# A residual plus bias, made by VectorE in attention and read back in feed-forward

## Chip, cores, metric

The program runs on one core of one Trainium2 chip. Its time is the device time of one execution in microseconds (us), lower is better. The engines are named as in the profile: PE is TensorE (PEld its weight loads), DVE is VectorE, ACT is ScalarE, POOL is GpSimd, SP is SyncE, which only issues DMAs; "SPq" rows are those issues.

## What is computed

A chain of four graph layers over 50000 nodes and 25000 edges, each followed by a residual and a normalization. The change touches the first layer alone, a graph transformer, and of it the end of the feed-forward part:

```python
scores = jnp.sum(q[src] * k[dst], axis=-1) / math.sqrt(D) + edge_bias
# softmax over the edges of each dst, weighted sum of v, out @ oW + ob
x = layer_norm(x + out, ln1_g, ln1_b)
h = x @ f1W + f1b
h = jax.nn.gelu(layer_norm(h, lnf_g, lnf_b), approximate=False)
h = h @ f2W + f2b
x = layer_norm(x + h, ln2_g, ln2_b)      # layer_norm(x, g, b) = (x - mu) * rsqrt(var + EPS) * g + b
...
x = _layernorm(x + _L0_gnn_ref(x, ...), axis=-1)
```

The last line adds the chain's input x to the layer's result. Since ln2_b is added last in that result, the kernel adds x + ln2_b (called xb) in one step: z = u * inverse + xb, where u is the centred row times ln2_g.

## The kernel before

Rows have 128 features. A tile is 512 rows, held as 128 partitions x 4 x 128 floats (256 KB). There are NT = 98 tiles of nodes and ET = 50 tiles of edges. The passes run one after the other: prepare (lists by counting), attention (attention_pass, about 110 to 768 us), feed-forward (ffn_pass, to about 1768 us), then back1, mean1, three gated layers and mean3, which the change leaves alone.

Every pass has one hand-written program for each engine. Within a pass, `over_tiles(engine, tiles, lag, step)` calls `step` once for each number `now`, and `tile_at(k)` in it is tile `now - k`; each engine carries out its step in the order in which it is written, and semaphore counts tie the engines together. `t.slot4` is the buffer n % 4, and a wait for a count of `t.n - 3` says that tile n - 4 has freed this buffer. `wait_alone` is the same wait ahead of a DMA issue, and everything that stands behind it on SyncE's queue stands still with it.

**Attention.** In step `now`, SyncE loads the list of edge ends of tile now (`idx`, L1261), edge features of tile now - 1 and cut of now - 2; the waits ahead of these concern buffers used some four tiles earlier. GpSimd issues eight gathers for tile now (L1282: four times 128 rows for the source, four for the destination), once idx has landed and the rows of tile now - 2 have been transposed by TensorE. TensorE transposes the rows, and in the next step makes q, k and v; VectorE in step `now` handles five stages of five tiles: the maxima of tile now - 3 (L1366 to L1379), the product q * k of tile now - 1 (L1385), att of now - 5 (L1392), sums of now - 3 (L1397 to L1409) and the output addition of now - 6 (L1416). Ahead of the loop SyncE loads eleven small weights of attention and then, by `up.load`, eleven for feed-forward, among them `up_idx`, the list of 98 x 4 pointers a partition, which is stored in HBM in runs of four integers.

**Feed-forward.** In step `now`, GpSimd issues four gathers (L1561), adds x and ln2_b for tile now - 10 (L1572), and raises the variances of four norms to the power -1/2 in one instruction (L1584), for which it waits for VectorE's L1717; VectorE's step has thirteen kinds of instructions, of them z (L1690), the only reader of xb. SyncE loads x of tile now and, a second time, x of tile now - 8 (`xr`, L1546), the latter once xb of tile now - 10 is made.

## Time and profile before

| | us |
|---|---|
| median of three timed runs | 5799.37 (5794.79 to 5803.73) |
| profiled execution | 5761.92 |
| its span | 5760.1 |
| attention, first gather to the start of feed-forward | 130.0 to 768.7 |
| feed-forward, its start to the next pass | 768.7 to about 1769.8 |
| busy over the span | PE 4126.6, DVE 3940.5, POOL 3502.3, ACT 2805.2 |

The profiled execution is 37 us shorter than the median. Shares over the whole span say little here, since the passes have different limits; each stage has to be read by itself, from windows and from the timeline. Where a timeline row carries "[4.25 <-POOL ...]", its engine had stood idle that long, and what is named came last; "issue" names nothing, and "remote" is a releaser that the records don't identify.

### The profile page before, as it was taken

To read this page: it belongs to the slowest core of one execution; us is meant where nothing else is said; L and a number is where in the kernel's file an instruction comes from. 1 tells how busy PE (TensorE), PEld (TensorE's weight loads), DVE (VectorE), ACT (ScalarE), POOL (GpSimd) and SP (SyncE) were. 2 spreads that over 40 slices of the span, in tenths; PEclk is the share of its full clock that TensorE was granted. 3 is DMA by queue.
4 is the path that set the end of the run, shared out by engine and by line. 5 is a ranking of instruction groups with operands and counts; after the bars stand their busy time and mean duration, and the time that the engine had idled before them with its cause. 6 is when DMAs were issued, how large, how long until landed. Compare 5 with 4: busy or idle time off the path is not lost. (4 is left out here: it accounts for less than half of the span.)

```text
span 5760.1 us, 75385 instructions
## 1 busy us (share of the span) xinstructions
PE 4126.6 (72%) x16190; PEld 2465.0 (43%) x16190; DVE 3940.5 (68%) x13570; ACT 2805.2 (49%) x6338; POOL 3502.3 (61%) x3137
## 2 busy tenths in 40 slices
PE   5666659999995555466564779967997669846644
PEld 3233335555552333355443445534443334346643
DVE  6567669999996444377774785557665888846643
ACT  0344437887782100076664445534444555536644
POOL 4677658888876888645556660056104757865456
PEclk8788879999997777777887999989998999978876
DMA  6233323333323444556664775457545666657621
GB/s 224 69 85 86 80 70 111 111 111 111 114 94 76 62 62 62 73 184 192 200 195 145 199 212 139 128 179 218 162 141 155 187 170 209 206 175 231 201 81 60
DMA packets 785242, 802.39 MB, mean 139 GB/s; under 512 B 138080, under 2 KB 551848, under 8 KB 784666
## 3 DMA queue, kind: packets, MB, share of 16 engines
q1 hardware_dynamic: 428922, 393.84, 23.9%
q0 software_dynamic: 117504, 209.42, 14.9%
q10 hardware_dynamic: 238368, 194.32, 10.0%
q8 instruction: 140, 2.29, 0.2%
q14 instruction: 308, 2.52, 0.1%
HBM read 445.32 MB, written 351.92 MB: 138 GB/s over the span
## 5 line engine op out<-in xcount | busy, mean ns | idle before, releaser
L476 PE MATMUL gate_bank<-gate_ht,gate_whh 128*128 128x512 f32 x1764 | 887.0, 618 | 61.2 <-DVE gate_n L546 36.1
L953 POOL DMA_INDIRECT xh<-mean_xh,node_pos x392 | 378.0, 964 | 323.2 <-DVE mean_xh L1009 173.0
L476 PEld LDWEIGHTS gate_bank<-gate_ht,gate_whh 128*128 128x128 f32 x1764 | 329.4, 198 | 465.8 <-issue 375.3
L2147 PE MATMUL back_ps_sums<-back_same,back_rows 128*128 128x512 f32 x400 | 287.2, 884 | 288.6 <-DMA back_rows<-x_a,back_idx 288.5
L1561 POOL DMA_INDIRECT ffn_rows<-att_sums,up_idx x392 | 395.0, 1008 | 109.0 <-issue 108.2
L291 POOL DMA_INDIRECT gate_rows<-h_a,by_pos x200 | 195.4, 977 | 431.9 <-POOLq L118 326.1
L472 PE MATMUL gate_bank<-by_rank,gate_win 128*128 128x512 f32 x882 | 435.2, 593 | 0.3 <-DVE by_rank L355 0.3
L612 ACT ACTIVATE gate_n<-gate_n,gate_b_ih 128x512 f32<-128x512 f32 x294 | 212.1, 721 | 399.0 <-issue 246.4
L1605 PE MATMUL ffn_ps_f<-ffn_hg,up_f 128*128 128x512 f32 x784 | 386.6, 595 | 3.2 <-ACT ffn_hg L1763 3.2
L1598 PE MATMUL ffn_ps_u<-ffn_xs_t,up_up_w 128*128 128x512 f32 x784 | 386.6, 595 | 1.1 <-issue 1.1
L2128 POOL DMA_INDIRECT back<-back_out,back_dest x200 | 324.6, 1623 | 67.9 <-issue 60.1
L323 PE MATMUL gate_bank<-gate_hot,gate_rows 128*128 128x128 f32 x1200 | 186.6, 304 | 236.5 <-issue 164.9
L601 ACT ACTIVATE gate_z<-gate_bank,gate_b_rz 128x512 f32<-128x512 f32 x294 | 200.4, 682 | 300.1 <-PE gate_bank L476 237.9
L1584 POOL TENSOR_TENSOR ffn_inv<-ffn_var,ffn_power 128x16 f32<-128x16 f32 x106 | 310.5, 2930 | 53.9 <-DVE ffn_var L1717 43.9
L585 ACT ACTIVATE gate_r<-gate_bank,gate_b_rz 128x512 f32<-128x512 f32 x294 | 200.0, 680 | 231.9 <-PE gate_bank L476 153.0
L1282 POOL DMA_INDIRECT attend_send<-in_x_in,attend_idx x200 | 213.7, 1069 | 144.4 <-issue 102.6
L2147 PEld LDWEIGHTS back_ps_sums<-back_same,back_rows 128*128 128x128 f32 x400 | 111.3, 293 | 432.4 <-DMA back_rows<-x_a,back_idx 262.2
L1763 ACT ACTIVATE ffn_hg<-ffn_ps_u,up_bf,up_gf 128x512 f32<-128x512 f32 x392 | 291.6, 767 | 9.8 <-PE ffn_ps_u L1598 8.0
L2210 ACT ACTIVATE back_sums<-back_ps_sums 128x512 f32<-128x512 f32 x50 | 29.9, 597 | 525.6 <-PE back_ps_sums L2147 518.0
L737 POOL DMA_INDIRECT out<-mean_y,node_at x196 | 188.3, 961 | 158.3 <-ACT mean_y L239 102.2
L291 POOL DMA_INDIRECT mean_rows<-x_c,by_pos x200 | 189.4, 947 | 146.9 <-PE mean_bank L323 92.2
L323 PEld LDWEIGHTS gate_bank<-gate_hot,gate_rows 128*128 128x128 f32 x1200 | 161.8, 209 | 268.5 <-issue 266.1
(270 smaller groups left out, 11744.6 us busy)
## 6 DMA issues: line engine op xcount, KB each, us to landing
mean_x<-x_a SPq DMA_DIRECT2D x196, 256.0 KB
back<-blank ACTq DMA_DIRECT2D x99, 264.0 KB, 4.5
mean_rows<-back SPq DMA_DIRECT2D x98, 264.0 KB
hp<-mean_xh SPq DMA_DIRECT2D x98, 264.0 KB
gate_x<-xh SPq DMA_DIRECT2D x98, 264.0 KB
gate_hot<-hot_rows SPq DMA_DIRECT2D x100, 256.0 KB
ffn_x<-in_x_in SPq DMA_DIRECT2D x98, 256.0 KB
ffn_xr<-in_x_in SPq DMA_DIRECT2D x98, 256.0 KB
```

Source lines behind the costliest of these rows:

```text
L291: self.nc.gpsimd.indirect_dma_start(out=self.rows[:, t.slot4, j, :], out_offset=None, in_=self.table[:, :], in_offset=bass.IndirectOffsetO ...
L323: last = self.nc.tensor.matmul(self.banks[t.n % len(self.banks)][:, j * P:(j + 1) * P], self.rows[:, t.slot4, j, 0:D], self.hot[:, t.slot4 ...
L472: last = nc.tensor.matmul(bank_[:, :], win[:, c * D:(c + 1) * D], g["by_rank"][:, t.tile * SUPER:(t.tile + 1) * SUPER], start=True, stop=n ...
L476: last = nc.tensor.matmul(bank_[:, :], whh[:, c * D:(c + 1) * D], ht[:, t.slot4, :], start=not inputs, stop=True)
L953: nc.gpsimd.indirect_dma_start(out=g["xh"][:, :], out_offset=bass.IndirectOffsetOnAxis(ap=pos_all[:, t.n, j:j + 1], axis=0), in_=xh[:, t.n ...
L1561: nc.gpsimd.indirect_dma_start(out=rows[:, t.slot4, j, :], out_offset=None, in_=g["att_sums"][:, :], in_offset=bass.IndirectOffsetOnAxis(a ...
L1584: nc.gpsimd.tensor_tensor(inv[:, now % 4, :, :].rearrange("p k j -> p (k j)"), var[:, now % 4, :, :].rearrange("p k j -> p (k j)"), power[ ...
L1598: nc.tensor.matmul(ps_u[(C * t.n + c) % 3][:, :], up_w[:, c * P:(c + 1) * P], xs_t[:, t.slot, :], start=True, stop=True).then_inc(up_made, 1)
L1605: last = nc.tensor.matmul(ps_f[:, :], f2[:, c, :], hg[:, c, :], start=c == 0, stop=c == C - 1)
L1763: nc.scalar.activation(hg[:, c, :], ps_u[(C * t.n + c) % 3][:, :], ACT.Gelu, bias=bf[:, c:c + 1], scale=gf[:, c:c + 1]).then_inc(gelu_done, 1)
L2128: nc.gpsimd.indirect_dma_start(out=g["back"][:, :], out_offset=bass.IndirectOffsetOnAxis(ap=dest[:, t.slot4, j:j + 1], axis=0), in_=out[:, ...
L2147: last = nc.tensor.matmul(ps_sums[t.slot][:, :], rows[:, t.slot4, j, :], same[:, t.slot, j, :], start=j == 0, stop=j == J - 1)
```

## The change

xb is now made in attention. SyncE there loads two node tiles of x in each step (nodes 2t and 2t + 1 for the edge tile t = now - 2), VectorE adds ln2_b at the end of its step (t = now - 3), and SyncE stores the results to a new table in HBM (t = now - 5). Both sides have four buffers. Feed-forward loads xb where it loaded x a second time, into four buffers instead of two, its load waiting for z of four tiles earlier, and GpSimd's addition is gone. The load of ln2_b moves to attention's first weights, and `up.load` from ahead of the loop to the end of SyncE's step 8.

```diff
@@ class UpWeights
-    PIECES, LOADS = FFN // P, 10
+    PIECES, LOADS = FFN // P, 9
...
-                           (self.g2[:, :], on_all(g["ln2_g"])), (self.b2[:, :], on_all(g["ln2_b"])),
+                           (self.g2[:, :], on_all(g["ln2_g"])),
@@ attention_pass
-        loads = 11
+        b2 = f.sb("b2", [P, D])
+        xin, xb = f.sb("xin", [P, 4, J, D]), f.sb("xb", [P, 4, J, D])
+        xin_loaded, xb_stored, xb_made = f.sems("xin_loaded", 4), f.sems("xb_stored", 4), f.sem("xb_made")
+        loads = 12
+
+        def nodes_at(behind, tile_at):
+            t = tile_at(behind)
+            return [Tile(n) for n in (2 * t.n, 2 * t.n + 1) if n < NT] if t else []
@@ attention_pass, block.sync
-                               (blocks[:, :, :], g["blocks_c"])):
+                               (blocks[:, :, :], g["blocks_c"]), (b2[:, :], on_all(g["ln2_b"]))):
                 sp.dma_start(dst_, src_, allow_slow_non_contiguous=True).then_inc(w_loaded, 16)
-            up.load(sp)
...
                     sp.dma_start(cut[:, t.slot4, :], row_tile(g["cut_dst"], t)).then_inc(cut_loaded[t.slot4], 16)
-            over_tiles(sp, ET, 2, step)
+                for x in nodes_at(2, tile_at):
+                    wait_alone(sp, xb_made, x.n - 3)
+                    sp.dma_start(flat(xin[:, x.slot4, :, :]), nm_tile(g["x_in"], x)).then_inc(xin_loaded[x.slot4], 16)
+                for x in nodes_at(5, tile_at):
+                    wait_alone(sp, xb_made, x.n + 1)
+                    sp.dma_start(nm_tile(g["xb"], x), flat(xb[:, x.slot4, :, :])).then_inc(xb_stored[x.slot4], 16)
+                if (t := tile_at(0)) and t.n == 8:
+                    up.load(sp)
+            over_tiles(sp, ET, 5, step)
+            for b in range(4):
+                sp.wait_ge(xb_stored[b], 16 * ((NT - b + 3) // 4))
@@ attention_pass, block.vector, at the end of step
+                for x in nodes_at(3, tile_at):
+                    wait(dve, xin_loaded[x.slot4], 16 * (x.u4 + 1))
+                    wait(dve, xb_stored[x.slot4], 16 * x.u4)
+                    nc.vector.tensor_tensor(xb[:, x.slot4, :, :], xin[:, x.slot4, :, :],
+                                            b2[:, :].unsqueeze(1).broadcast_to([P, J, D]), ALU.add).then_inc(xb_made, 1)
@@ ffn_pass, block.sync
                 if t := tile_at(8):
-                    wait_alone(sp, xb_done, t.n - 1)
-                    sp.dma_start(flat(xr[:, t.slot, :, :]), nm_tile(g["x_in"], t)).then_inc(xr_loaded[t.slot], 16)
+                    wait_alone(sp, z_done, t.n - 3)
+                    sp.dma_start(flat(xb[:, t.slot4, :, :]), nm_tile(g["xb"], t)).then_inc(xb_loaded[t.slot4], 16)
@@ ffn_pass, block.gpsimd
-                if t := tile_at(10):
-                    wait(pool, xr_loaded[t.slot], 16 * (t.u + 1))
-                    wait(pool, z_done, t.n - 1)
-                    nc.gpsimd.tensor_tensor(xb[:, t.slot, :, :], xr[:, t.slot, :, :],
-                                            b2[:, :].unsqueeze(1).broadcast_to([P, J, D]), ALU.add
-                                            ).then_inc(xb_done, 1)
@@ ffn_pass, block.vector
                 if t := tile_at(11):
                     wait(dve, roots_done, roots_by(t, LN2))
-                    wait(dve, xb_done, t.n + 1)
+                    wait(dve, xb_loaded[t.slot4], 16 * (t.u4 + 1))
@@ build
+    g["xb"] = dram("xb", [NP, D])
```

In the program the new instructions stand as follows. SyncE, before, around edge tiles 5 and 6; attend_received and attend_sent are the landings of gathers four tiles earlier, s_made, drop_done and top_done are stages of tiles four or five earlier:

```order
L1261 DMA attend_idx<-in_edge_blocks 128x8 [waits attend_sent1,attend_received1]
L1265 DMA attend_edge_t<-in_edge_attr_t 32x512 [waits attend_s_made]
L1270 DMA attend_cut<-cut_dst 128x512
L1261 DMA attend_idx<-in_edge_blocks 128x8 [waits attend_sent2,attend_received2]
L1265 DMA attend_edge_t<-in_edge_attr_t 32x512 [waits attend_s_made]
```

SyncE, after, from the last two loads of `up.load` through step 9 to the start of step 10; xb_made counts VectorE's new additions:

```order
L1132 DMA up_g<-in_ln_g 128x128
L1132 DMA up_idx<-ptr_dst 128x98x4
L1267 DMA attend_idx<-in_edge_blocks 128x8 [waits attend_sent1,attend_received1]
L1271 DMA attend_edge_t<-in_edge_attr_t 32x512 [waits attend_s_made]
L1276 DMA attend_cut<-cut_dst 128x512 [waits attend_drop_done,attend_top_done]
L1279 DMA attend_xin<-in_x_in 128x512 [waits attend_xb_made] x2
L1282 DMA xb<-attend_xb 128x512 [waits attend_xb_made] x2
L1267 DMA attend_idx<-in_edge_blocks 128x8 [waits attend_sent2,attend_received2]
```

The list of edge ends now stands behind four transfers of 256 KB, of which the first two wait for additions of VectorE; and `up.load`, which stood ahead of tile 0's list, stands ahead of tile 9's. On VectorE a step of attention, after, in full:

```order
L1382 COPY attend_top<-attend_top 128x1
L1386 SCALAR_TENSOR_TENSOR attend_top<-attend_cut,attend_top,attend_s 128x512
L1390 TENSOR_TENSOR attend_arg<-attend_s,attend_top 128x512
L1392 TENSOR_TENSOR attend_drop<-attend_top,attend_cut 128x512
L1395 TENSOR_TENSOR attend_arg<-attend_drop,attend_top 128x512
L1401 SCALAR_TENSOR_TENSOR attend_qk<-attend_ps_k,attend_kb,attend_q 128x512
L1408 SCALAR_TENSOR_TENSOR attend_att<-attend_inv,attend_num 128x512
L1413 TENSOR_TENSOR attend_pv<-attend_v,attend_ex 128x512
L1418 SCALAR_TENSOR_TENSOR attend_den<-attend_ex,attend_den 128x512
L1425 SCALAR_TENSOR_TENSOR attend_num<-attend_ex,attend_num,attend_pv 128x512
L1432 TENSOR_TENSOR attend_out<-attend_ps_out,attend_ob 128x512
L1447 TENSOR_TENSOR attend_xb<-attend_xin,attend_b 128x512 x2
```

Its first eleven rows are those of before; the last is new.

## Rows read from the trace of the kernel before

**Rows 1.** The stages by windows: stretch, time, busy and instructions by engine, PEclk, DMA share, GB/s.
```profile
120.00:765.00 645.00, 405.79 (x1314) 208.75 (x1314) 418.26 (x562) 256.64 (x400) 420.11 (x400) 0.79 0.32 77
...
900.00:1650.00 750.00, 735.22 (x2845) 402.50 (x2844) 731.49 (x3319) 599.31 (x1186) 650.81 (x474) 1.00 0.35 112
```

**Rows 2.** GpSimd's instructions in feed-forward: start, duration, line, operands, idle before and its releaser.
```profile
1201.23 2.93 POOL L1584 TENSOR_TENSOR ffn_inv<-ffn_var,ffn_power 128x16 f32<-128x16 f32 x1
...
1209.26 1.28 POOL L1572 TENSOR_TENSOR ffn_xb<-ffn_xr,up_b 128x512 f32<-128x512 f32 x1
1210.66 2.93 POOL L1584 TENSOR_TENSOR ffn_inv<-ffn_var,ffn_power 128x16 f32<-128x16 f32 x1
```

**Rows 3.** VectorE's variances in feed-forward: timeline in mid-stage and in the drain; groups of 900:1650.
```profile
1210.30 0.28 DVE L1717 TENSOR_SCALAR ffn_var<-ffn_mv 128x16 f32<-128x16 f32 x1 [0.19 <-issue]
...
1684.36 0.17 DVE L1717 TENSOR_SCALAR ffn_var<-ffn_mv 128x16 f32<-128x16 f32 x1 [0.19 <-issue]
...
1693.71 0.17 DVE L1717 TENSOR_SCALAR ffn_var<-ffn_mv 128x16 f32<-128x16 f32 x1 [0.19 <-issue]
...
L1717 DVE TENSOR_SCALAR ffn_var<-ffn_mv 128x16 f32<-128x16 f32 x79 | 26.5, 335 | 15.0 <-issue 14.9 <-DVE ffn_mv L1659 0.2
```

**Rows 4.** Attention: the gathers' and the products' instructions: minimum/median/maximum ns, first and last start.
```profile
L1282 POOL DMA_INDIRECT attend_send<-in_x_in,attend_idx x200: 941/947/1952, 130.0 to 713.0; - x100
...
L1385 DVE SCALAR_TENSOR_TENSOR attend_qk<-attend_ps_k,attend_kb,attend_q x50: 743/745/752, 147.3 to 733.7; 128x512 f32<-128x512 f32 x50
```

**Rows 5.** Attention, timeline of VectorE: products before and after a stall, and of two undisturbed steps.
```profile
408.50 0.74 DVE L1385 SCALAR_TENSOR_TENSOR attend_qk<-attend_ps_k,attend_kb,attend_q 128x512 f32<-128x512 f32 x1
...
425.17 0.69 DVE L1416 TENSOR_TENSOR attend_out<-attend_ps_out,attend_ob 128x512 f32<-128x512 f32 x1 [12.34 <-remote]
...
432.21 0.75 DVE L1385 SCALAR_TENSOR_TENSOR attend_qk<-attend_ps_k,attend_kb,attend_q 128x512 f32<-128x512 f32 x1 [2.92 <-remote]
...
459.82 0.74 DVE L1385 SCALAR_TENSOR_TENSOR attend_qk<-attend_ps_k,attend_kb,attend_q 128x512 f32<-128x512 f32 x1
...
464.08 0.66 DVE L1416 TENSOR_TENSOR attend_out<-attend_ps_out,attend_ob 128x512 f32<-128x512 f32 x1
...
468.09 0.74 DVE L1385 SCALAR_TENSOR_TENSOR attend_qk<-attend_ps_k,attend_kb,attend_q 128x512 f32<-128x512 f32 x1
```

**Rows 6.** Attention, timeline: an index load, its gathers much later, a gather beside a scan.
```profile
400.32 0.30 SPq L1261 DMA_DIRECT2D attend_idx<-in_edge_blocks  x1
...
433.13 1.25 POOL L1282 DMA_INDIRECT attend_send<-in_x_in,attend_idx  x1 [3.75 <-issue]
...
435.71 1.28 DVE L1402 TENSOR_TENSOR_SCAN attend_den<-attend_ex,attend_den 128x512 f32<-128x512 f32 x1
435.93 1.81 POOL L1282 DMA_INDIRECT attend_send<-in_x_in,attend_idx  x1 [0.30 <-issue]
```

**Rows 7.** Start of back1, timeline of SyncE's queue and GpSimd: an index load behind large loads.
```profile
1770.16 0.43 SPq L2095 DMA_DIRECT2D back_mask<-in_mask_c  x1
...
1771.10 0.43 SPq L2101 DMA_DIRECT2D back_idx<-in_edges  x1
...
1776.46 1.02 POOL L2118 DMA_INDIRECT back_rows<-x_a,back_idx  x1 [11.79 <-DMA back_idx<-in_edges]
```

**Rows 8.** Start of attention, timeline; and a window over the landing of the lists.
```profile
119.54 0.43 SPq L1132 DMA_DIRECT2D up_idx<-ptr_dst  x1
120.01 7.48 SPq L1261 DMA_DIRECT2D attend_idx<-in_edge_blocks  x2
...
130.03 1.18 POOL L1282 DMA_INDIRECT attend_send<-in_x_in,attend_idx  x1 [41.76 <-DMA attend_idx<-in_edge_blocks]
...
120.00:130.00 10.00, 0.00 (x0) 0.00 (x0) 0.00 (x0) 0.00 (x0) 0.00 (x0) 0.50 0.93 47
```

**Rows 9.** Groups of instructions, page and 200:700 us: busy, mean ns of one, idle before.
```profile
L1572 POOL TENSOR_TENSOR ffn_xb<-ffn_xr,up_b 128x512 f32<-128x512 f32 x98 | 125.4, 1280 | 2.1
...
L1374 DVE TENSOR_TENSOR attend_arg<-attend_s,attend_top 128x512 f32<-128x512 f32 x42 | 29.1, 693 | 1.5
```

More of the change, by code:

```diff
@@ L1113, in __init__ @@
         self.gf, self.bf = sb("gf", [P, C]), sb("bf", [P, C])
-        self.g2, self.b2 = sb("g2", [P, D]), sb("b2", [P, D])
+        self.g2 = sb("g2", [P, D])
         (self.w_loaded, self.total_done, self.mean_done, self.centred, self.gap_done, self.spread_done,
@@ L1491, in ffn_pass @@
         up_w, gram, f2, idx = up.up_w, up.gram, up.f2, up.idx
-        g1, b1, f2b, gf, bf, g2, b2 = up.g1, up.b1, up.f2b, up.gf, up.bf, up.g2, up.b2
+        g1, b1, f2b, gf, bf, g2 = up.g1, up.b1, up.f2b, up.gf, up.bf, up.g2
         one = f.sb("one", [P, 1])
@@ L1495, in ffn_pass @@
         a, xh = f.sb("a", [P, 4, J, D]), f.sb("xh", [P, 4, J, D])
-        xr, u, xb, z, y, xs = (f.sb(s, [P, 2, J, D]) for s in ("xr", "u", "xb", "z", "y", "xs"))
+        xb = f.sb("xb", [P, 4, J, D])
+        u, z, y, xs = (f.sb(s, [P, 2, J, D]) for s in ("u", "z", "y", "xs"))
         xa_t, xs_t, y2t = (f.sb(s, [P, 2, SUPER]) for s in ("xa_t", "xs_t", "y2t"))
@@ L1515, in ffn_pass @@
                                "xs_done", "xs_turned", "xs_t_done", "up_made", "gelu_done", "f2_made", "y2t_done",
-                               "y2_turned", "u_done", "xb_done", "z_done", "shift_done", "y_done", "vars_done",
+                               "y2_turned", "u_done", "z_done", "shift_done", "y_done", "vars_done",
                                "roots_done"))
```

6 lines of the change are left out of this document (3 added, 3 removed).

## The prediction, made before the changed kernel was run

> **What bounds the kernel now.** The change touches two stages, so I read the windows by stage first, and the shares of the page hardly. In feed-forward PE and DVE are both busy for 98% of 750 us [rows 1]; in attention no engine is above 65% (DVE 418 and POOL 420 of 645 us), so there it is chains and waits that count.
>
> Feed-forward. From one power instruction of GpSimd to the next it is 9.43 us, and the next starts 0.12 us after GpSimd's addition xb has ended [rows 2]. In between stands VectorE's variance: begun at 1210.30 it lasts until 1210.58, 0.04 us after xb's end at 1210.54, and the power starts 0.08 us later [rows 2, 3]. In the drain, where xb no longer runs beside it, the same instruction takes 0.17 us, and a step of VectorE with the same work takes 9.35 us (1684.36 to 1693.71) [rows 3]. Its mean in mid-stage is 335 ns; and 79 of them in 750 us are 9.49 us a tile, since every dozen tiles one is late by about 1 us. So GpSimd's addition sets the beat there, but by a hair: behind it stand VectorE with 9.35 and PE with 735.2 / 79 = 9.31 us a tile [rows 1].
>
> Attention. Fifty products L1385 start between 147.3 and 733.7 [rows 4], 11.97 us a tile. Undisturbed, VectorE's step takes 8.27 us without a gap (459.82 to 468.09), and then there are stalls: the product of 408.50 is followed by one at 432.21, with 12.3 and 2.9 us of idle time whose releaser the records don't name [rows 5]. Such stalls come every four to five tiles; all of them together hold 586.4 - 49 x 8.27 = 181 us. GpSimd needs (420.1 / 400 + 0.30) x 8 = 10.8 us for a tile's gathers [rows 1, 6]. So between stalls VectorE catches up with GpSimd, and during stalls GpSimd works ahead: the list for the tile that is gathered from 433.13 on was issued at 400.32 [rows 6]. This store of work ahead is what holds attention to 11.97 us.
>
> **Part 1, feed-forward without GpSimd's addition.** 98 additions of 1.28 us go [rows 9]. The next limit is VectorE at 9.35 us, against 9.49: 0.14 us for each of the some 88 tiles between fill and drain, **-12 us**. Bounds: 9.43 against 9.38 gives -4; down to PE's 9.31 gives -16. SyncE's load of xb replaces one of the same size, its buffers are four instead of two, and z is its only reader: at nothing, hidden behind three steps of 9.4 us; if that cover were gone, the loads would be late by some us once, not in each tile.
>
> **Part 2, the start of attention.** Ten loads and up_idx stood ahead of tile 0's list: eleven issues of 0.47 us (119.54 to 120.01 is the last), then the list's at 120.01; the gathers start at 130.03, while DMA was 93% busy with only 47 GB/s, that is with up_idx's short runs [rows 8]. After the change one load stands there instead of eleven, so the list is issued 10 x 0.47 us earlier, at 115.3. Its landing I take from back1, where a list behind a 1 MB load landed 5.4 us after its issue [rows 7]: 120.7, **-9 us**. Bounds -5 (the landing of 10.0 us remains) and -14 (it is under 1 us).
> The same loads now stand ahead of tile 9's list. Ten issues are 4.7 us, and the list behind up_idx needs 10.0 us [rows 8] instead of 5.4: 9.3 us later than its neighbours. VectorE and GpSimd then hold less than a step of work ahead (part 4), so I take it as paid: **+9**, bounds 0 and +15.
>
> **Part 3, the additions on VectorE and their neighbours.** 98 additions with both inputs in SBUF; the like L1374 takes 0.69 us, [rows 9], back to back about 0.65: 64 us of VectorE's time, 1.3 in each step. They stand at the end of the step, so its next maxima and product come later. GpSimd's gathers feel them: a gather that started at 435.93 beside a scan with two SBUF inputs took 1.81 us instead of 0.95, and ended 0.75 us after that scan [rows 4, 6]. Gathers average 1.05 over a base of 0.95 [rows 1, 4], 0.8 us a tile for some 7.5 us of VectorE's work; 1.3 us more should cost in proportion 0.14 us a tile, 7 us, at most one half addition, 0.35 us, 17. I take **+8**, bounds 0 and +17.
> Against this term stands a rule of the Trainium skill (SBUF — State Buffer, section Who interferes with whom): a tensor_tensor with two SBUF inputs takes only the read side of the pair that VectorE and GpSimd share, and descriptor generation needs the write side. By it the additions would not touch the gathers, and the sum would be 8 us smaller; the row of 435.93 shows a gather held until after a two-input scan, though a scan is another instruction than this addition.
>
> **Part 4, the list of edge ends waits for VectorE.** This is the largest term. In SyncE's step `now` the loads of x wait for xb_made of four nodes earlier; for nodes 2(now-2) and 2(now-2)+1 that is VectorE's step now - 1, finished. Behind them on the queue stand two stores and then the list of tile now + 1, and behind the list GpSimd. So the gathers of tile n start only after VectorE's step n - 2 has ended and 1 MB of transfers and the list have gone through, some 5.8 us later by the case of back1 [rows 7]. The list's lead of 33 us is gone. A loop of three steps: gathers 10.8; to the product 7.3 (tile 0: eight gathers end at 140.0, product at 147.3) [rows 4, 8]; rest of the step [rows 5] 6.2 (product to the end of the output addition, 459.82 to 464.74, 4.9, and 1.3 for xb); list 5.8; together 30.1, or 10.0 a step. That is under GpSimd's 10.8, so in quiet stretches nothing is lost. But nothing is left either, to absorb a stall: VectorE can no longer catch up at 8.27, since its next gathers start late. Each stall then costs what its step exceeds 10.8 by. Summed over the 49 steps between the products of [rows 4] (23.7 at [rows 5] is one of eight over 16 us) this excess is 109 us: 49 x 10.8 + 109 = 638 against 586, +52. If each stall is paid in full, 49 x 10.8 + 181 = 710, +124. On the other side, VectorE's own 64 us alone, without any effect on the lists, would give +64 where it works without a gap, and next to nothing where the stalls' 181 us swallow them. I take **+70**: the lockstep's 52 and a part of the additions that it doesn't contain, since they lengthen stalled steps too. Bounds 0 and +124.
>
> **Sum.** -12 - 9 + 9 + 8 + 70 = +66 us. Against the profiled execution, 5761.9, that is 5828; it is 37 us under the median of the timed runs, and the timed result is to be compared with those: 5799.4 + 66 = **5865 us**.
>
> **The rivals.**
> *Hidden and faster.* Attention leaves VectorE idle for 227 of 645 us [rows 1]. If the stalls are a fixed amount of time in which VectorE only waits, its backlog grows by 1.3 us a step and is worked off within them, and if the lists land in 2 or 3 us, GpSimd keeps its pace. Then parts 3 and 4 are 0, part 2 is -9 and part 1 -12: 5778. It decides whether the loop of three steps, with a stall in it, stays under 3 x 11.97 = 36 us; with 30.1 there are 6 us to spare, and the stall of [rows 5] is 12.3 and more. That speaks against it. The Trainium skill (GPSIMD Engine Reference, section Engine selection) says to put elementwise work on VectorE, as GpSimd takes about twice as long with two inputs; here that is 0.69 against 1.28 us, and this rival is the case in which the rule alone decides.
> *Mostly hidden.* The additions go into stalls, but each of a dozen stalls gives 1 to 3 us on to the lists: some +25 in attention for parts 2 to 4 beyond the start's -9, which returns what the other parts gain: 5799 - 12 - 9 + 25 = 5803.
> *Full price.* Every stall is paid, +124, and more DMA traffic (50 MB) makes none shorter: 5799 - 12 + 8 + 124 = 5919. For it speaks that the loads and stores of 1 MB a step stand on the same queue as the lists; against it, that a stall may fall together with a wait for gathers.
> That the change doesn't do what it says is only open for feed-forward: if the beat of 9.43 is VectorE's own, part 1 is 0, and every case is 12 us later.
>
> **Chances.** Forecast (5811 to 5890, likeliest 5865) 0.57; full price (5890 and over) 0.22; mostly hidden 0.09; faster 0.12. The range leaves out the faster case and the end of the full price: 5797 to 5925. Some 0.2%, 12 us, is what a measurement of this kernel can tell from no change: faster 0.12, same 0.09, slower 0.79.
>
> **What would show it.** Right: in attention the list's issue stands right behind xb's stores and the gathers start with an idle time whose releaser is the list; GpSimd's lead is gone; products 12.5 to 14 us apart in the mean; first gather near 120; one gap of about 10 us at tile 9. In feed-forward L1717 takes 0.17 us throughout and the steps are 9.35 to 9.38 us. Wrong: products still 8.3 us apart behind a stall (then part 4 fell), stalls shorter than before, or an unchanged 9.43 in feed-forward.

## The result, and the profile after

The changed kernel takes 5814.68 us (median of 20 runs, 5803.21 to 5828.23), the kernel before beside it 5803.43 us (20 runs): a ratio of 1.0020, with a 95% interval of 1.0014 to 1.0026, or **+11 us** (8 to 15). The forecast was +66.

The profiled execution of the changed kernel took 5819.05 us, its span 5817.3. The one of before was 42 us under its median and 33 under the lowest of its 20 timed runs, and the chip it ran on is not on record, so the two can't be compared as wholes; stage by stage they can, with the caution that they may come from two chips. A stage begins here at its first instruction on GpSimd, read from the timeline. "Rest" is everything from back1 to GpSimd's last instruction, which the change doesn't touch:

| profiled execution (us) | to attention | attention | feed-forward | rest |
|---|---|---|---|---|
| before | 130.0 | 638.7 | 1007.8 | 3981.0 |
| after | 118.2 | 685.3 | 994.9 | 4016.3 |
| difference | -11.8 | +46.6 | -12.9 | +35.3 |

The touched stages come to +22 us, against +11 timed; the +35 of the rest is no effect of the change, as the table of the experiments shows.

Windows by stage, to be held against [rows 1]: stretch, time, busy and instructions of PE, PEld, DVE, ACT and POOL, PEclk, DMA share, GB/s.

```profile
150.00:795.00 645.00, 428.54 (x1269) 245.73 (x1269) 473.98 (x655) 256.26 (x394) 405.57 (x375) 0.76 0.53 152
900.00:1650.00 750.00, 745.56 (x2890) 409.15 (x2889) 730.62 (x3368) 609.02 (x1203) 608.41 (x402) 1.00 0.35 114
```

In feed-forward POOL has fewer instructions and PE is busy for 745.6 us of 750 where it was 735.2: the beat is now PE's and VectorE's. The group of variances, which answers to the last row of [rows 3]:

```profile
L1733 DVE TENSOR_SCALAR ffn_var<-ffn_mv 128x16 f32<-128x16 f32 x80 | 14.0, 175 | 15.9 <-issue 15.9
```

In attention, the start and tile 9 on SyncE's queue and GpSimd (timeline):

```profile
114.64 0.91 SPq L1267 DMA_DIRECT2D attend_idx<-in_edge_blocks  x2
...
118.21 1.18 POOL L1298 DMA_INDIRECT attend_send<-in_x_in,attend_idx  x1 [30.33 <-DMA attend_idx<-in_edge_blocks]
...
229.10 0.43 SPq L1132 DMA_DIRECT2D up_idx<-ptr_dst  x1
229.69 8.11 SPq L1267 DMA_DIRECT2D attend_idx<-in_edge_blocks  x1
...
239.80 1.00 POOL L1298 DMA_INDIRECT attend_send<-in_x_in,attend_idx  x1 [11.83 <-DMA attend_idx<-in_edge_blocks]
```

And a step in the middle, which answers to [rows 6]: the list is issued right behind the pairs of xin and xb, and GpSimd gathers with it 4 us later, where in [rows 6] it was 33. From tile 5 on, the time from a list's issue to its first gather is 1 to 10 us in the changed kernel, and 22 to 35 in before.

```profile
560.56 0.93 SPq L1279 DMA_DIRECT2D attend_xin<-in_x_in  x2
561.58 0.86 SPq L1282 DMA_DIRECT2D xb<-attend_xb  x2
562.59 0.33 SPq L1267 DMA_DIRECT2D attend_idx<-in_edge_blocks  x1
...
566.58 1.76 POOL L1298 DMA_INDIRECT attend_send<-in_x_in,attend_idx  x1 [0.71 <-issue]
```

The products, to be held against the last row of [rows 4] (minimum/median/maximum ns, first and last start):

```profile
L1401 DVE SCALAR_TENSOR_TENSOR attend_qk<-attend_ps_k,attend_kb,attend_q x50: 742/744/752, 135.5 to 767.3; 128x512 f32<-128x512 f32 x50
```

That is 631.8 us for 49 steps, 12.89 a step; before it was 11.97. So the lockstep came as forecast, but it cost 0.92 us a step and not some 1.8.

### The profile page after: what moved, and what is told of

Read it like the earlier page. It is cut to its first block and busy times, and to the rows that moved or that the text cites. A ratio compares the mean times of both kernels' runs of the same rounds, so it can differ in the third digit from the quotient of the medians.

```text
span 5817.3 us, 75772 instructions
## 1 busy us (share of the span) xinstructions
PE 4178.1 (72%) x16190; PEld 2517.6 (43%) x16190; DVE 3980.1 (68%) x13668; ACT 2807.9 (48%) x6338; POOL 3446.2 (59%) x3039
## 5 line engine op out<-in xcount | busy, mean ns | idle before, releaser
L1583 POOL DMA_INDIRECT ffn_rows<-att_sums,up_idx x392 | 448.8, 1145 | 109.0 <-issue 108.2
L1779 ACT ACTIVATE ffn_hg<-ffn_ps_u,up_bf,up_gf 128x512 f32<-128x512 f32 x392 | 291.4, 767 | 10.1 <-PE ffn_ps_u L1614 9.6
L546 DVE SCALAR_TENSOR_TENSOR gate_n<-gate_bank,gate_b_hh,gate_r 128x512 f32<-128x512 f32 x294 | 219.2, 746 | 88.7 <-ACT gate_r L585 32.9
```

The lines of the kernel that those rows point to most:

```text
L1583: nc.gpsimd.indirect_dma_start(out=rows[:, t.slot4, j, :], out_offset=None, in_=g["att_sums"][:, :], in_offset=bass.IndirectOffsetOnAxis(a ...
L1779: nc.scalar.activation(hg[:, c, :], ps_u[(C * t.n + c) % 3][:, :], ACT.Gelu, bias=bf[:, c:c + 1], scale=gf[:, c:c + 1]).then_inc(gelu_done, 1)
```

## The experiments

Five chips took part, in the order of the experiments: A to E. Since the kernel before ran beside every kernel, ratios are safe; the chips themselves differ. (Each chip was used for one group of runs only, so what is put down to a chip below could also belong to its group.) Before takes 5452 us on A and 5449 on E, but 5757, 5762 and 5804 on B, C and D. The ratios have 95% intervals of about +/- 0.001. All stages below are from the profiled executions, as in the table above.


The theories on what attention loses, as the expectations name them: **A**, the lists that wait for VectorE, as far as GpSimd has no work ahead to cover it; **B**, VectorE's additions themselves; **C** and **E**, the transfers, or these and the additions by longer stalls; **D**, the lists' way behind VectorE and the transfers as a pace of its own; **F** and **G**, instruction fetches behind the stalls; **H**, loads and stores merely spread otherwise over the steps.

| kernel (chip) | time, us | ratio | to attention | attention | feed-forward | rest |
|---|---|---|---|---|---|---|
| before_again (A) | 5455.1 | 1.0004 | 130.0 | 590.3 | 1006.9 | 3717.7 |
| ffn_alone (A) | 5441.9 | 0.9976 | 130.2 | 592.1 | 994.2 | 3723.9 |
| additions_alone (A) | 5458.5 | 1.0009 | 131.7 | 588.6 | 1008.6 | 3720.4 |
| lists_free (A) | 5432.5 | 0.9959 | 118.4 | 598.0 | 995.1 | 3719.6 |
| after_again (B) | 5773.0 | 1.0028 | 118.9 | 682.7 | 994.7 | 3978.9 |
| loads_ahead (B) | 5768.7 | 1.0016 | 131.0 | 661.2 | 994.9 | 3973.9 |
| lockstep_alone (B) | 5775.6 | 1.0035 | 129.9 | 660.0 | 1006.9 | 3973.5 |
| one_column (B) | 5771.1 | 1.0023 | 118.8 | 689.5 | 994.7 | 3978.0 |
| after_third (C) | 5777.9 | 1.0027 | 118.6 | 676.8 | 995.7 | 3971.7 |
| lists_free_2 (C) | 5746.6 | 0.9972 | 118.2 | 646.5 | 995.2 | 3970.8 |
| additions_alone_2 (C) | 5769.0 | 1.0014 | 131.2 | 644.9 | 1012.0 | 3979.0 |
| three_a_step (C) | 5736.4 | **0.9959** | 118.6 | 642.9 | 995.6 | 3976.6 |
| after_fourth (D) | 5818.9 | 1.0031 | 118.9 | 685.0 | 995.4 | 4003.7 |
| three_a_step_2 (D) | 5783.1 | **0.9962** | 118.7 | 650.6 | 995.4 | 4007.5 |
| pe_padded (D) | 5795.9 | 0.9990 | 130.2 | 647.2 | 1006.9 | 4011.5 |
| act_padded (D) | 5804.5 | 0.9998 | 129.9 | 645.1 | 1007.6 | 4021.7 |
| wait_put_back (E) | 5451.4 | 1.0001 | 118.4 | 616.1 | 995.1 | 3714.6 |
| after_fifth (E) | 5502.1 | **1.0093** | 118.8 | 668.6 | 995.0 | 3715.6 |

### The kernel before once more, and parts of the change alone

Before, unchanged:

> The kernel before, unchanged, for a second profiled execution. The first took 5761.9 us and the changed kernel's 5819.1, while the medians of the timed runs are only 11 us apart; stages that the change does not touch differ by 35 us between these two profiles. If that is scatter of single executions, this one has an attention of 630 to 650 us from its first gather to feed-forward's first instruction of GpSimd, feed-forward 1005 to 1008, and the rest (back1 onwards) some 20 to 40 us longer than 3983.6. If the rest is again 3984 +/- 5, the change does something to the later stages, and my account by stages has to be made anew.

The rest was neither: 3718 us, 263 less than in the first profile; this chip takes 5452 us for the kernel where the first pair's took 5803. The rest of all eighteen kernels goes by the chip (3715 to 3724 on A and E, 3971 to 3979 on B and C, 4004 to 4022 on D), and not by whether the change is in them. So the +35 of the first pair of profiles is no effect of the change. Before's 3981.0 there fits B and C and the changed kernel's 4016.3 fits D, so the two profiles may well come from two chips; then part of their +46.6 in attention is the chips' too. And attention on this chip has none of the stalls. GpSimd's waits in 150:700 us of before_again (us in total, times, longest):

```profile
POOL attend_send L1282 <- issue: 58.5, 192, 0.3
POOL attend_recv L1282 <- issue: 58.5, 192, 0.3
```

Its products, in the columns of [rows 4]:

```profile
L1385 DVE SCALAR_TENSOR_TENSOR attend_qk<-attend_ps_k,attend_kb,attend_q x50: 742/744/751, 147.0 to 684.2; 128x512 f32<-128x512 f32 x50
```

No wait of GpSimd is longer than its usual 0.3 us: there it is GpSimd that gives the beat, 10.83 us a tile from gather to gather, and VectorE follows with (684.2 - 147.0) / 49 = 10.96.

Feed-forward alone:

```diff
-                if t := tile_at(10):
-                    wait(pool, xr_loaded[t.slot], 16 * (t.u + 1))
-                    wait(pool, z_done, t.n - 1)
-                    nc.gpsimd.tensor_tensor(xb[:, t.slot, :, :], xr[:, t.slot, :, :],
...
-                    sp.dma_start(flat(xr[:, t.slot, :, :]), nm_tile(g["x_in"], t)).then_inc(xr_loaded[t.slot], 16)
+                    sp.dma_start(flat(xb[:, t.slot4, :, :]), nm_tile(g["x_in"], t)).then_inc(xb_loaded[t.slot4], 16)
```

> The kernel before, with feed-forward's part of the change alone: GpSimd's addition is left out, and VectorE's z takes x without the second norm's bias, so this part of the computation is missing. Attention is the one of before. Expected by part 1: -12 to -14 us against before (feed-forward 993 to 995 us instead of 1007), 5803.4 - 13 = 5790. If part of the profiles' gain of 13 us was scatter: -4 to -8.

0.9976 (0.9966 to 0.9987), -11 us timed and 994.2 against 1006.9 us in the profile: the gain is all there, without anything new in attention. What brought it is GpSimd's addition that is gone, together with the two more buffers and the other wait of the load that replaces it; these weren't tried one by one.

The additions alone, in attention of the kernel before:

```diff
+                for x in nodes_at(3, tile_at):
+                    wait(dve, xb_made, x.n - 3)
+                    nc.vector.tensor_tensor(xb[:, x.slot4, :, :], xin[:, x.slot4, :, :],
+                                            b2[:, :].unsqueeze(1).broadcast_to([P, J, D]), ALU.add).then_inc(xb_made, 1)
```

> The kernel before, with 98 additions of the same shape added to VectorE's steps at the same place in attention, two in each step, from a buffer that is set once into another that nobody reads: no load, no store, nothing new for SyncE to wait for. Feed-forward is the one of before. Theory A: 0 to +8 us, the 64 us of VectorE's work vanish in its idle time. Rival B: +35 to +45, 5840 to 5850. Rival C: 0 to +8.

> The same kernel as additions_alone (98 additions in attention of the kernel before, no transfers, no new wait for the lists), which without stalls made attention 1.7 us shorter and the whole 1.0009 of before. With stalls, theory A: 0 to +5 us; rival E: +20 to +45, 1.004 to 1.008. Without stalls: 1.001 again.

1.0009 and 1.0014, by these ratios 5 and 8 us; the second is above the 0 to +5 expected and far below rival E's 20. Of the first the profile shows 1.7 us in front of attention (one load and a memset more) and nothing in attention (588.6 against 590.3). So nearly all of the 64 us of VectorE's work vanish in its idle time, with stalls and without. Rivals B (VectorE's work itself) and E (additions lengthen stalls) fall.

### The list of edge ends

SyncE's loads of x two steps later and its stores one step later; nothing else is changed:

```diff
-                for x in nodes_at(2, tile_at):
+                for x in nodes_at(4, tile_at):
                     wait_alone(sp, xb_made, x.n - 3)
...
-                for x in nodes_at(5, tile_at):
+                for x in nodes_at(6, tile_at):
```

> The changed kernel with the loads of x two steps later on SyncE (4 steps behind instead of 2) and the stores of xb one step later (6 instead of 5). The list of tile now+1 then stands behind VectorE's step now-3 instead of now-1; additions and transfers are all still there. Theory A (what attention lost, 46.7 us in the profiles, it lost to the lists that wait for VectorE): attention falls from 686 back to 640 to 650, the list's lead of two to three tiles returns, and the time is 5814.7 - 40 = 5775, ratio to before 0.995. Rival B (it lost it to VectorE's additions themselves, 1.3 us a step in the chain): 5810 to 5818, attention 680 to 690. Rival C (the megabyte of loads and stores in each step slows the gathers): the same as B in time, and the gathers longer than 1.05 us or landing later.

> The same kernel as in the run lists_free, which took 0.9959 of before where before takes 5452 us and has no stalls in attention. Where before takes 5757 us or more and has them: theory A (attention loses 20 us to lists that wait for VectorE, 11 us to tile 9's list behind the ten loads, and next to nothing to additions and transfers) expects attention at 640 to 648 us against 639, start -12, feed-forward -12, ratio 0.997. Rival E (what attention loses there it loses to the transfers and additions, which lengthen the stalls, whatever the lists do): attention 660 to 685, ratio 1.000 to 1.004. On a chip without stalls: 0.996 again.

0.9959 and 0.9972, as theory A has it. All additions and all 50 MB of transfers are still there, and attention takes 598.0 us on A and 646.5 on C, where after_third beside it takes 676.8. So rival C (the transfers) falls as well, unless it matters where in the step they stand, which is H. GpSimd's waits in lists_free_2 (200:700 us) name no list any more:

```profile
POOL attend_send L1298 <- issue: 95.4, 168, 3.5
POOL attend_recv L1298 <- issue: 54.6, 169, 2.0
```

Against it the changed kernel itself, on three more chips:

> The changed kernel, unchanged. In the runs just made, the kernel before takes 5452 us instead of 5803; its attention 590 us instead of 639, with GpSimd's gathers following each other at 0.30 us and none of the stalls with the releaser 'remote' (89.5 us of VectorE's idle time in the first profile, none here). Theory A (the lists' wait for VectorE costs what a stall exceeds GpSimd's step by, and nothing in quiet stretches): without stalls the loop of 10.0 us a step stays under GpSimd's 10.9, attention keeps 590 plus 9 for tile 9's list, and the sum is 5452 - 12 (feed-forward) - 12 (start) + 9 = 5437 or so, ratio 0.997; the start, feed-forward and tile 9 alone show. Rival D (the lists' way through a megabyte of transfers is longer than GpSimd's step in every tile): attention 610 to 640, ratio 1.001 to 1.006, and gathers that wait for the list in most tiles.

> The changed kernel again, for the comparison on this chip. With stalls: 1.002 to 1.003 of before, attention 683 to 686 us. Without stalls, theory A: start -12, feed-forward -12, tile 9 +11, the lists free since 10.0 us a step is under GpSimd's 10.8: 0.997 to 0.998. Rival D (the lists' way through the transfers sets the pace whether there are stalls or not): attention 625 us or more, 1.001 to 1.004.

> The changed kernel again. Where before takes 5757 to 5762 us and stalls: 1.0027 +/- 0.001, attention 677 to 685 us. Where before takes 5452 us and doesn't stall in attention: theory A: 590 + 11 (tile 9) in attention, start -12, feed-forward -12, ratio 0.997 to 0.998; rival D (the lists' way behind VectorE and a megabyte sets a pace of its own): attention 625 us or more, 1.001 to 1.004.

1.0028, 1.0027 and 1.0031 on B, C and D, all three with stalls in before. With lists_free_2 and after_third on one chip, the place of the list and tile 9 are worth 0.0055 of 5762, 32 us.

The wait alone, in the kernel before:

```diff
                     wait_alone(sp, received[t.slot4], 64 * t.u4)
+                    wait_alone(sp, out_done, t.n - 7)
                     sp.dma_start(idx[:, t.slot4, :, :].rearrange("p j c -> p (j c)"),
```

> The kernel before with one more wait on SyncE: the list of tile n is issued only when VectorE has ended the output addition of its step n - 2. No addition, no load and no store is added; feed-forward and the start are those of before. Theory A, without stalls: 0 to +5 us. Where stalls come (as in the first profile): +30 to +52. Rival D: 0 here, since no transfer stands between the wait and the list.

1.0035, +20 us, on a chip with stalls: under the 30 to 52 expected. Its products run from 147.2 to 755.1, 12.41 us apart. GpSimd waits for the list at 10 tiles between 150 and 770 us, 60.1 us in all. Its steps are uneven: from tile 10 on, two tiles take 17 to 32 us from list to list, where the changed kernel on E takes 24 to 26 from tile 11 on. Since no transfer stands before it, the list reaches GpSimd 2.66 us after its issue (timeline):

```profile
482.74 0.33 SPq L1262 DMA_DIRECT2D attend_idx<-in_edge_blocks  x1
...
485.40 0.94 POOL L1283 DMA_INDIRECT attend_send<-in_x_in,attend_idx  x1 [6.23 <-DMA attend_idx<-in_edge_blocks]
```

The ten loads back ahead of the loop:

```diff
+            up.load(sp)
+
             def step(tile_at):
...
-                if (t := tile_at(0)) and t.n == 8:
-                    up.load(sp)
```

> The changed kernel with the ten loads of feed-forward's constants back ahead of the loop. Part 2 alone is undone: the first gather moves from 118.2 back to 130, and tile 9's gathers no longer start some 10 us late. If the gap at tile 9 is paid, as I took it: the same time as the changed kernel, +/- 3 us. If the gap is absorbed: 9 to 12 us slower than the changed kernel.

1.0016 against 1.0028 for the changed kernel beside it: 4 us faster by the medians, with intervals that overlap, so the two can't be told apart. The products show how the move loses what it gains: after_again is 12.4 us ahead at tile 0 (135.9 against 148.3), 7.8 ahead at tile 8 (242.3, 250.1), and 3.0 behind at tile 9 (266.1, 263.1). So tile 9 costs 11 us. It is 10.8 behind at the last product, which single executions may scatter.

The additions cut to one column, with all waits and transfers:

```diff
-                    nc.vector.tensor_tensor(xb[:, x.slot4, :, :], xin[:, x.slot4, :, :],
-                                            b2[:, :].unsqueeze(1).broadcast_to([P, J, D]), ALU.add).then_inc(xb_made, 1)
+                    nc.vector.tensor_tensor(xb[:, x.slot4, 0, 0:1], xin[:, x.slot4, 0, 0:1],
+                                            b2[:, 0:1], ALU.add).then_inc(xb_made, 1)
```

> The changed kernel with each addition of x and the bias cut to one column of 512; the transfers, the waits and the lists' place behind them are unchanged. What is stored as x plus bias is then a constant, so this part of the computation is missing. Theory A without stalls: 0 to -3 us against the changed kernel, since VectorE has idle time enough. Rival B: -30 or more. Rival D: the same as the changed kernel, less what VectorE's shorter step brings its lists forward (1.3 us a step, up to -60 if the lists set the pace).

1.0023 against 1.0028, within both intervals: nothing gained, on a chip with stalls. Its steps are uneven again (8 to 24 us), so what the shorter step gives may be taken by stalls that the lockstep can't absorb; that isn't shown, since no one_column ran where nothing stalls. By itself this run speaks against rival D, which had up to 60 us for it.

### Where nothing stalls: the loop itself

```diff
+                    wait_alone(sp, out_done, t.n - 7)
```

in lists_free, ahead of the list, as in lockstep_alone; and the changed kernel beside it.

> lists_free with one wait more on SyncE: the list of tile n is issued only when VectorE has ended the output addition of its step n - 2, as in lockstep_alone. Additions, transfers and their places are those of lists_free. Theory A (the lists' wait is what attention loses, and it also exposes tile 9's list): where before stalls, attention goes from 643 to 650 us back to 675 to 685, ratio 1.002 to 1.003; where it doesn't, from 598 to 598 to 612. Rival H (what lists_free gained came from loads and stores spread otherwise over the steps): attention stays within 8 us of 646 (or 598), ratio 0.996 to 0.998.

> The changed kernel, beside wait_put_back. Where before stalls: 1.002 to 1.003, attention 677 to 685. Where before takes 5452 us: theory A 0.997 to 0.998 with attention near 601; rival D 1.001 to 1.004 with attention of 625 us or more.

This was the surprise of the study. On E, where before has no stalls, **the changed kernel is 0.93% slower, 53 us**, and not faster: theory A, which had the lists' wait free in quiet stretches, falls there, and rival D is right in kind, though it had 1.001 to 1.004. The wait for VectorE's output addition alone brings attention from 598.0 (lists_free on A) to 616.1, with GpSimd waiting for a list 24 times and 15 us in all; that is 4 us over theory A's range, and H, which had attention unchanged, falls; the list's place behind the additions and four transfers, and tile 9, bring it to 668.6. GpSimd's wait for the list in after_fifth (150:770 us; us in total, times, longest):

```profile
POOL attend_send L1298 <- DMA attend_idx<-in_edge_blocks: 71.8, 38, 14.8
```

and its products:

```profile
L1401 DVE SCALAR_TENSOR_TENSOR attend_qk<-attend_ps_k,attend_kb,attend_q x50: 742/744/752, 135.8 to 749.7; 128x512 f32<-128x512 f32 x50
```

It waits for the list at 38 tiles. Since no stall disturbs it, the loop can be read off line by line. Timeline of after_fifth, one turn of it:

```profile
584.48 0.63 SPq L1267 DMA_DIRECT2D attend_idx<-in_edge_blocks  x1
...
589.18 0.94 POOL L1298 DMA_INDIRECT attend_send<-in_x_in,attend_idx  x1 [2.85 <-DMA attend_idx<-in_edge_blocks]
...
596.07 0.33 SPq L1267 DMA_DIRECT2D attend_idx<-in_edge_blocks  x1
...
598.39 0.94 POOL L1298 DMA_INDIRECT attend_recv<-in_x_in,attend_idx  x1 [0.30 <-issue]
...
601.42 1.12 PE L1337 MATMUL attend_ps_send<-ident,attend_send 128*128 128x128 f32 x4 [4.19 <-DMA attend_send<-in_x_in,attend_idx]
603.18 1.92 PE L1348 MATMUL attend_ps_out<-attend_ow,attend_att 128*128 128x128 f32 x8
...
605.13 0.69 DVE L1432 TENSOR_TENSOR attend_out<-attend_ps_out,attend_ob 128x512 f32<-128x512 f32 x1 [2.90 <-PE attend_ps_out L1348]
605.74 1.28 DVE L1447 TENSOR_TENSOR attend_xb<-attend_xin,attend_b 128x512 f32<-128x512 f32 x2
...
606.50 0.93 SPq L1279 DMA_DIRECT2D attend_xin<-in_x_in  x2
607.52 0.86 SPq L1282 DMA_DIRECT2D xb<-attend_xb  x2
608.53 0.38 SPq L1267 DMA_DIRECT2D attend_idx<-in_edge_blocks  x1
```

List to first gather 4.70 us, eight gathers 10.15, landing and to the transposes 2.09, transposes 1.76, PE's output product 1.95, VectorE's output addition and the first half of xb 1.37, the four transfers' issues 2.03: 24.05 us. In that time two tiles have gone by, for the list of the tile between was issued at 596.07. So the loop gives 12.0 us a tile by this turn, and (749.7 - 326.0) / 34 = 12.46 in the mean from product 15 on. On B and C the changed kernel's mean over the same products is 12.45 (764.5 - 341.1 and 758.4 - 335.2, over 34), in the first pair 12.63 and on D 12.59. **The change has nearly one pace on every chip**, 12.45 to 12.63, though its stalls haven't all gone where before has them. What it costs goes by the pace of before: 10.96 where nothing stalls, 11.97 where it does.

One thing more stands in the loop. TensorE had stood idle for 4.19 us before the transposes, and in this time its granted clock fell from 1.00 (2.4 GHz) to 0.50 (1.2 GHz). The transposes and the product of 603.18 ran at the lower level (windows of after_fifth, in the columns of [rows 1]; the third number from the right is the clock):

```profile
596.00:598.00 2.00, 1.23 (x3) 0.29 (x2) 1.97 (x4) 1.19 (x3) 1.70 (x2) 1.00 0.97 357
600.00:601.00 1.00, 0.00 (x0) 0.00 (x0) 1.00 (x2) 0.00 (x0) 0.74 (x1) 0.50 0.70 169
603.00:604.00 1.00, 1.00 (x6) 1.00 (x5) 0.00 (x0) 0.57 (x2) 0.69 (x2) 0.50 0.25 57
```

The same product in before, where the clock of 410 to 412 us is 1.00 (timeline):

```profile
410.71 1.06 PE L1332 MATMUL attend_ps_out<-attend_ow,attend_att 128*128 128x128 f32 x8
```

Of the output products that the traces show as one row of eight between 150 and 700 us, 31 of 36 took over 1.7 us in after_fifth, 28 of 46 in before_again and 2 of 39 in before. By these rows the lower clock makes the turn above 0.9 us longer in the product alone (an estimate, 1.92 less 1.06).

### A version that beats both

lists_free with three additions in each of the first 33 steps; xin and xb have six buffers instead of four, and the waits count accordingly:

```diff
-            return [Tile(n) for n in (2 * t.n, 2 * t.n + 1) if n < NT] if t else []
+            return [Tile(n) for n in range(3 * t.n, 3 * t.n + 3) if n < NT] if t else []
...
-                    wait_alone(sp, xb_made, x.n - 3)
+                    wait_alone(sp, xb_made, x.n - 5)
```

> lists_free with three additions in each of VectorE's first 33 steps instead of two in each of 49, and six buffers instead of four. In the run without stalls GpSimd gave the beat (10.8 us a tile) and the last product came 29.4 us behind the last gathers' start, against 23.7 in before: VectorE's last steps, which also hold feed-forward's first work, grew by the additions. Expected: these 6 us are won back, since 8.3 + 3 x 0.65 = 10.2 us stays under 10.8; ratio 0.995 without stalls, and 0.001 under lists_free_2 with them. Rival: three in a step press VectorE's step over GpSimd's where a step also waits, and nothing is won or 5 to 10 us lost.

> The same kernel as three_a_step, which gave 0.9959 of before. Again 0.995 to 0.997, with stalls or without: it has the changed kernel's feed-forward and start, and its lists stand behind VectorE's step now-3.

0.9959 (0.9947 to 0.9971) and 0.9962 (0.9948 to 0.9976): by these ratios 24 and 22 us faster than before, and by the medians 42 and 36 us faster than the changed kernel beside it, on chips with stalls. Against lists_free_2 on its chip it is 0.0013 faster; the intervals of the two overlap. It also shows how stalls and quiet steps trade. VectorE's products around the last additions and well after them (timeline):

```profile
499.67 0.75 DVE L1401 SCALAR_TENSOR_TENSOR attend_qk<-attend_ps_k,attend_kb,attend_q 128x512 f32<-128x512 f32 x1
509.74 0.74 DVE L1401 SCALAR_TENSOR_TENSOR attend_qk<-attend_ps_k,attend_kb,attend_q 128x512 f32<-128x512 f32 x1
519.80 0.74 DVE L1401 SCALAR_TENSOR_TENSOR attend_qk<-attend_ps_k,attend_kb,attend_q 128x512 f32<-128x512 f32 x1
529.87 0.74 DVE L1401 SCALAR_TENSOR_TENSOR attend_qk<-attend_ps_k,attend_kb,attend_q 128x512 f32<-128x512 f32 x1
542.17 0.74 DVE L1401 SCALAR_TENSOR_TENSOR attend_qk<-attend_ps_k,attend_kb,attend_q 128x512 f32<-128x512 f32 x1
558.67 0.74 DVE L1401 SCALAR_TENSOR_TENSOR attend_qk<-attend_ps_k,attend_kb,attend_q 128x512 f32<-128x512 f32 x1
...
647.15 0.74 DVE L1401 SCALAR_TENSOR_TENSOR attend_qk<-attend_ps_k,attend_kb,attend_q 128x512 f32<-128x512 f32 x1
655.65 0.74 DVE L1401 SCALAR_TENSOR_TENSOR attend_qk<-attend_ps_k,attend_kb,attend_q 128x512 f32<-128x512 f32 x1
...
681.61 0.75 DVE L1401 SCALAR_TENSOR_TENSOR attend_qk<-attend_ps_k,attend_kb,attend_q 128x512 f32<-128x512 f32 x1
706.50 0.74 DVE L1401 SCALAR_TENSOR_TENSOR attend_qk<-attend_ps_k,attend_kb,attend_q 128x512 f32<-128x512 f32 x1
```

With three additions the quiet steps are 10.1 us and the long one 16.5; without them they are 8.3 and 24.9. Five products together take 59.0 us (499.67 to 558.67) and 59.4 us (647.15 to 706.50) all the same. That is no fixed period: over all stretches of five from product 15 on it is 54 to 66 us here and 53 to 70 in before. What holds is the mean. From product 15 on the products are 11.87 us apart in before, 11.89 in additions_alone_2, 11.83 in lists_free_2, 11.91 and 11.99 in the two runs of this kernel. Where VectorE has more to do the quiet steps grow and the stalls shrink by as much.

### What the stalls are

50 empty instructions on PE, and 30 on ACT, in each step of attention of the kernel before:

```diff
+                    for _ in range(50):
+                        pe.nop(nofuse=True)
```

> The kernel before with 50 empty instructions of PE in each step of attention, behind the output products. They compute nothing; PE's instructions in attention about double, and with them its fetches of 16 KB (11 in the stage). Theory F (the stalls without a visible releaser are tied to PE's instruction fetches): 20 to 24 fetches, stalls every two to three tiles instead of every five, attention some 30 to 120 us longer than 639 where stalls occur. Rival: stalls every four to six tiles as before; attention 0 to 20 us longer, for the time that PE spends on the empty instructions.

> The same for ACT: 30 empty instructions in each of its steps in attention, behind the copies of the turned rows. Theory G (the stalls are tied to ACT's instruction fetches of 8 KB): more and closer stalls, attention 30 to 120 us longer where stalls occur. Rival: stalls every four to six tiles, attention 0 to 20 us longer.

0.9990 and 0.9998: no change. But the DMA records show 11 instruction packets of 16 KB and 20 of 8 KB in attention, with the empty instructions and without. What the experiment was to double stayed as it was, so theories F and G are not tested by it; it tells only that these instructions, as written, cost nothing there. **The cause of the stalls stays open**: none are in the kernels profiled on A and E, some in all of those on B, C and D, and their releaser isn't in the records.

## Why the prediction was wrong, step by step

- **Feed-forward (part 1), -12: right.** 1007.8 to 994.9 us, and 994 to 996 in every kernel that has it. The variance takes 0.175 us throughout, as the drain of before had shown. That it comes from feed-forward's own part and not from attention's is shown by ffn_alone.
- **The start (part 2), -9: right, the size a little low.** -11.8: the list was issued at 114.64 (forecast 115.3) and landed in 3.6 us, not 5.4. **Tile 9, +9: right**, 11 us by loads_ahead, and paid, as taken. The gain of the start and the loss at tile 9 cancel: by time loads_ahead and the change can't be told apart.
- **Additions beside gathers (part 3), +8: wrong, it is nothing.** The gathers average 1.042 and 1.053 us in additions_alone and additions_alone_2, 1.047 in before_again, 1.051 in before. In the changed kernel they average 1.07 to 1.08, but in lists_free and lists_free_2, with the same additions, 1.050 and 1.038. That isn't the lockstep by itself, since lockstep_alone has 1.032 and three_a_step, without it, 1.080; what makes it stays open. The row of 435.93 in [rows 6] showed a gather held by a scan; a plain addition doesn't hold one: in after_fifth the 30 gathers that overlap one of the new additions and no scan average 0.95 us, the 177 that overlap a scan 1.20. The Trainium skill (SBUF — State Buffer, section Who interferes with whom) says that an addition with both inputs in SBUF takes the read side alone of the shared pair, and infers that generating descriptors needs the write side; these rows agree. The forecast had the rule and left it for a row of another instruction.
- **The list's wait (part 4), +70: the right mechanism, the wrong working.** The wait for VectorE costs: lists_free_2 takes it away and 32 us (with tile 9) go, lockstep_alone adds it alone and 20 come. From 46.6 us in attention 11 belong to tile 9, and some 35 are left where 70 were forecast; by lists_free_2 and lockstep_alone it is only some 20. In the forecast's own terms, 52 stood for the lockstep, and 18 for additions "since they lengthen stalled steps too". The 18 measured next to nothing (additions_alone_2), and the 52 measured 20 to 35. Two steps of the working failed.
  First, "a loop of three steps ... 30.1, or 10.0 a step. That is under GpSimd's 10.8, so in quiet stretches nothing is lost". I closed the loop through the product, which VectorE makes one step after the gathers. But PE's output product stands in its program right behind the transposes of the newest tile, and VectorE's output addition of the same step waits for it. The additions and with them SyncE wait behind that. That loop has two steps, not three; it measures 24.05 us, 12.0 a tile, over GpSimd's 10.8. Quiet stretches lose the most: +53 us on E.
  Second, "each stall then costs what its step exceeds 10.8 by", on top. A stall shrinks by as much as the quiet steps grow (three_a_step). The cost is then the difference of two paces: (12.89 - 11.97) x 49 = 45 us, tile 9 in it, in the first pair, and ((749.7 - 135.8) / 49 - 10.96) x 49 = 77 us on E. These two only restate the products' times; what supports the account is the loop of 12.0 us, which was read from single rows.
  But the forecast's idea that a lockstep leaves nothing to absorb a stall isn't refuted. lockstep_alone goes at 12.33 us from product 15 on, though its wait with all additions and transfers added, where nothing stalls, gives 11.40 (wait_put_back), and before's own pace is 11.87. The larger of these two doesn't reach 12.33, so there a wait and stalls do add up. How the cost of the change on B, C and D divides between the loop's pace and this is not shown.
- **The rivals.** "Hidden and faster" asked whether the loop with a stall stays under 36 us, and so measured the wrong loop as well. "Mostly hidden", 5803, had the size within 12 us but not the mechanism: it let the stalls swallow the additions (they do) and a dozen of them pass something on to the lists, where E shows that the loop costs most with no stall at all. That its number came so close is luck. "Full price" fell, since stalls shrink and aren't paid in full.
- The sum of the right values, -12.9 - 11.8 + 11 + 0 + 35.6, is +22 us by the profiles; the medians of the timed runs are 11 to 16 us apart where before stalls. Most of the gap seems to come with before's first profile. On D, where the padded kernels do before's work in attention, after_fourth against pe_padded and act_padded is +15 and +17 us over the three stages, and +14 timed; attention's part of it is 38 to 40 and not 46.6.

Open: the cause of the stalls; why one_column, with 1.2 us less in the loop, gains nothing where stalls are; and which share the wait on xb_made and which the transfers ahead of the list have of the 52 us between wait_put_back and after_fifth, tile 9 in it.

## What to carry to other kernels

When a change puts a wait ahead of something that others need, look for every loop that closes through it, and take the one with the most time per step: follow each engine's program order, since an instruction that only stands behind another one closes a loop as well as a data dependence does. If stalls shrink as the quiet steps grow, add up some periods before pricing them: here the mean pace held where single stalls didn't, and most of the price was the difference of two paces. Don't take it for a rule, since lockstep_alone cost more than either pace explains. The remedy was cheap: the same loads and stores, one or two steps later on the queue, so that they wait for nothing that is late.

## What the runs showed of the hardware

- The same program takes 5449 and 5452 us on two chips and 5757 to 5804 on three others. Of its two profiles the spans are 5447.6 and 5760.1 us. Attention differs by 48 us (stalls), the first mean stage by 109 (665.0 against 555.8), feed-forward by 1. What a change costs can depend on it: the changed kernel loses 0.3% on the slower chips and 0.9% on E.
- A list of 12,544 runs of 16 bytes (up_idx) holds the queue: the next load on it, 4 KB, shows 8.11 us in the records where others show 0.33, and is used 10.1 us after its issue.
- An index list of 4 KB reached GpSimd 2.66 us after its issue with nothing ahead of it on the queue, and 4.70 us with four transfers of 256 KB ahead.
- Of GpSimd's gathers in after_fifth, those beside a scan of VectorE's took 1.20 us in the mean and those beside an addition and no scan 0.95.
- TensorE's granted clock fell from 1.00 to 0.50 while it stood idle for 4.19 us in after_fifth, and its output product, 1.06 us at the full clock, took 1.92.
